# Attention probabilities: six of eight key blocks transposed by DMA, the fp16 cast on ACT, two tiles' PSUM evictions as one

## The reference

```
c_kv = x @ w_dkv; c_q = x @ w_dq
k = concat(rope(x @ w_kr) to all heads, c_kv @ w_uk)      # 16 heads, 64 + 128
q = concat(rope(c_q @ w_qr), c_q @ w_uq)
v = c_kv @ w_uv                                           # 16 heads x 128
attn = softmax(q k^T / sqrt(192)); out = (attn v) @ w_o
x = layernorm(x + out)
w1q, w3q, w2q = ternary(w1), ternary(w3), ternary(w2)     # hidden 682
x = layernorm(x + (silu(x w1q^T) * (x w3q^T)) @ w2q^T)
```

## Time and profile before

| | us |
|---|---|
| median of 3 runs | 1011.03 (1008.86 to 1012.56) |
| the profiled execution | 1020.05 |
| its span in the profile | 1017.9 |
| one pair of heads (300.44 to 343.86) | 43.42 |
| attention, batch 0 and 1 | about 105 to 452 and 584 to 931 |

### The profile page before, as it was taken

The page is one execution under the profiler, slowest core; times in us unless marked ns, Lnnn a source line. Parts: engine busy times, 40 slices in busy tenths (PEclk is TensorE's granted clock), DMA queues, the critical chain, the costliest instruction groups (busy, mean ns, idle before and its releaser), DMA issues.

```text
span 1017.9 us, 18739 instructions
## 1 busy us (share of the span) xinstructions
PE 965.2 (95%) x5622; PEld 696.4 (68%) x5622; DVE 741.0 (73%) x1164; ACT 603.5 (59%) x1036; POOL 605.3 (59%) x643
## 2 busy tenths in 40 slices
PE   7989999999999999998979989999999999997985
PEld 3548766766676766667866866766666676675874
DVE  1756788888888888863456678888888888885455
ACT  2636777777767666751333587766766766764132
POOL 0007777777777777760340787777777777674034
PEclk9799999999999999999989999999999999999998
DMA  9553755545454544566100575655545455457101
GB/s 260 148 217 88 143 103 101 94 95 103 93 96 93 106 94 96 100 140 261 44 23 22 120 129 94 102 100 99 96 89 103 93 97 99 94 103 190 59 1 42
DMA packets 288450, 107.62 MB, mean 106 GB/s; under 512 B 274492, under 2 KB 282512, under 8 KB 287376
## 3 DMA queue, kind: packets, MB, share of 16 engines
q1 hardware_dynamic: 286944, 97.03, 46.1%
q10 hardware_dynamic: 880, 7.86, 2.1%
q0 software_dynamic: 576, 2.10, 0.6%
HBM read 23.85 MB, written 7.60 MB: 31 GB/s over the span
## 4 chain that ended last, share of the span: by engine, by line
PE 73%; issue 10%; DVE 8%; POOL 4%; ACT 2%; DMA 2%; SPq 1%; ACTq 0%; POOLq 0%; DVEq 0%
PE Sa L1045 17%; PE Sb L1045 15%; PE Oa L1072 15%; PE Tb L1054 5%; PE Ta L1054 4%; DVE nmax L753 4%; PE Sb L1096 2%; DVE Q_lo L767 2%; PE Sa L1096 2%; POOL g_lo L415 1%; PE Ob L1082 1%; PE Sb L1172 1%; DMA xr<-in_L_attn_x_dram 1%; POOL P_parts L383 1%; PE Sa L1015 1%
## 5 line engine op out<-in xcount | busy, mean ns | idle before, releaser
L753 DVE TENSOR_REDUCE nmax<-Sa 128x1 f32<-128x1024 f32 x128 | 155.9, 1218 | 78.5 <-PE Sa L1045 77.1
L383 POOL TENSOR_TENSOR P_parts<-probs_a,P_parts 128x512 f16<-128x512 f32 x128 | 169.6, 1325 | 23.5 <-POOL P_parts L380 23.5
L753 DVE TENSOR_REDUCE nmax<-Sb 128x1 f32<-128x1024 f32 x128 | 156.0, 1219 | 20.0 <-PE Sb L1045 20.0
L383 POOL TENSOR_TENSOR P_parts<-probs_b,P_parts 128x512 f16<-128x512 f32 x128 | 149.2, 1166 | 23.9 <-POOL P_parts L380 23.9
L439 ACT ACTIVATE PT_hi<-Ta 128x512 f16<-128x512 f32 x128 | 76.3, 596 | 110.6 <-PE Ta L1054 110.6
L380 POOL TENSOR_SCALAR P_parts<-probs_a 128x512 f16<-128x512 f32 x128 | 80.8, 631 | 75.8 <-ACT probs_a L538 70.4
L380 POOL TENSOR_SCALAR P_parts<-probs_b 128x512 f16<-128x512 f32 x128 | 80.9, 632 | 51.1 <-ACT probs_b L538 48.9
L351 POOL TENSOR_TENSOR turned<-qmul 128x1024 f32<-128x1024 f32 x16 | 38.1, 2404 | 112.2 <-DVE qmul L748 112.2
L1045 PE MATMUL Sb<-K_hi,Q_hi 128*128 128x512 f32 x256 | 91.0, 436 | 7.8 <-ACT probs_b L538 4.0
L1045 PE MATMUL Sa<-K_hi,Q_hi 128*128 128x512 f32 x256 | 93.0, 444 | 0.0
L538 ACT ACTIVATE probs_b<-Sb,nmax 128x1024 f32<-128x1024 f32 x64 | 71.4, 1116 | 33.0 <-DVE nmax L756 33.0
(11 more groups left out here) (298 smaller groups left out, 2118.6 us busy)
## 6 DMA issues: line engine op xcount, KB each, us to landing
QO<-turned SPq DMA_DIRECT2D x64, 128.0 KB, 2.3
TT<-ternary SPq DMA_DIRECT2D x2, 2304.0 KB, 11.5
PT_dma<-P_parts SPq DMA_TRANSPOSE x256, 3.0
ternary<-tern ACTq DMA_DIRECT2D x1, 2304.0 KB, 8.2
wo<-in_L_attn_w_o_dram SPq DMA_DIRECT2D x4, 512.0 KB, 8.1
xq<-in_L_attn_x_dram SPq DMA_DIRECT2D x2, 1024.0 KB, 9.7
wq_high<-Wq_hi ACTq DMA_DIRECT2D x1, 2048.0 KB, 12.7
Wvo_lo<-wvo_low ACTq DMA_DIRECT2D x2, 1024.0 KB, 5.7
```

Of the source, the lines that this page charges most:

```text
L383: nc.gpsimd.tensor_tensor(P_parts[:, n % DEEP, 1, :], src, P_parts[:, n % DEEP, 0, :], ALU.subtract).then_inc(part_lo, 1)
L753: nc.vector.tensor_reduce(nmax[:, n % 4:n % 4 + 1], SS[n % 2][:, :], AX.X, ALU.max, negate=True).then_inc(row_max, 1)
```

## The change

- KP = 2 key blocks stay with TensorE, KD = 6 go by DMA. `transpose_probs` makes two turns a tile instead of four, and two tiles share one PSUM bank (Ta for tiles 0 and 1, Tb for 2 and 3, and so on). ACT evicts and DVE subtracts once for two tiles, after the odd one, 512 columns as before.
- The fp16 cast of the DMA's blocks, now 768 columns, moves from POOL (`split_probs`) to ACT (`part_high`), behind the exponential of the next tile. With it moves the wait for the DMA transpose of four tiles before. POOL keeps the subtraction, of 768 columns (`low_probs`).
- A DMA transpose has 12 blocks instead of 8. TensorE waits for the transposes of a half at key block 2 instead of 4, which is after tile 3 or 11 instead of 5 or 13.
- `P_parts` is larger and reaches into the first four tiles of Wq_lo. These go to HBM in the setup (`wq_low`, 0.5 MB, after waits for `prod_lo` and `qr_lo`) and come back behind Wq_hi after batch 0. Some buffers lie elsewhere.
- The waits that POOL had ahead of the first pair (`q_ps`, `wq_out`) are now waits of ACT at its tile 0 (`wq_out`, `rope_sum`).

```diff
 
 
 DEEP = 4
-KD = KT // 2
+KP = 2
+KD = KT - KP
+SPILL = 4
 EXP0, PT0, PTL0, PV0, OUT0, ROW0, Y0, STORED0, READ0 = 2, DEEP, 2, 2, 1, 1, 2, 1, 1
 
 
...
     ternary = nc.dram_tensor("ternary", [P, W], F, kind="Internal").ap()
 
     wq_high = nc.dram_tensor("wq_high", [P, H * 2 * P], F, kind="Internal").ap()
+    wq_low = nc.dram_tensor("wq_low", [P, SPILL * 2 * P], F, kind="Internal").ap()
     wvo_low = nc.dram_tensor("wvo_low", [P, PAIRS * D], F, kind="Internal").ap()
 
     ctx = ExitStack()
...
                 sp.dma_start(tcos[:, :], cos).then_inc(proj_in, 16)
                 sp.dma_start(tsin[:, :], sin).then_inc(proj_in, 16)
                 if b:
-                    sp.wait_ge(wq_in, 16)
+                    sp.wait_ge(wq_in, 32)
                     sp.sem_inc(wq_ready, 1)
                 for g in range(GROUPS):
                     if g == 3:
...
                 if b + 1 < B:
                     for r in range(DEEP):
                         sp.wait_ge(part_in[r], 16 * TILES * PAIRS // DEEP)
-                    sp.wait_ge(wq_out, 16)
+                    sp.wait_ge(wq_out, 32)
                     sp.dma_start(Wq_hi[:, :, :, :].rearrange("p h c m -> p (h c m)").bitcast(F), wq_high).then_inc(wq_in, 16)
+                    sp.dma_start(Wq_lo[:, 0:SPILL].rearrange("p h c m -> p (h c m)").bitcast(F), wq_low).then_inc(wq_in, 16)
 
 
         @block.gpsimd
...
                     else:
                         nc.gpsimd.tensor_copy(O_parts[:, pair_row, cols], QO[:, pair_row + 1, cols]).then_inc(out_hi, 1)
 
-                def split_probs(tile, n, reused):
-
-                    src = probs[n % DEEP][:, KD * P:S]
-                    hold(pool, exp_done, EXP0 + tile + 1)
-                    if reused is not None:
-                        hold(pool, part_in[n % DEEP], reused)
-                    nc.gpsimd.tensor_scalar(P_parts[:, n % DEEP, 0, :], src, 1.0, 1.0, ALU.mult,
-                                            ALU.mult).then_inc(part_hi, 1)
+                def low_probs(tile, n):
+
                     hold(pool, part_hi, tile + 1)
-                    nc.gpsimd.tensor_tensor(P_parts[:, n % DEEP, 1, :], src, P_parts[:, n % DEEP, 0, :],
-                                            ALU.subtract).then_inc(part_lo, 1)
+                    nc.gpsimd.tensor_tensor(P_parts[:, n % DEEP, 1, :], probs[n % DEEP][:, KP * P:S],
+                                            P_parts[:, n % DEEP, 0, :], ALU.subtract).then_inc(part_lo, 1)
 
                 def pair_pool(p, first, last):
                     pair = b * PAIRS + p
                     for n in range(TILES):
                         h = n // 8
-                        split_probs(pair * TILES + n, n,
-                                    None if first and n < DEEP else 16 * (pair * TILES // DEEP + n // DEEP))
+                        low_probs(pair * TILES + n, n)
                         if n % 8 == 0 and not (first and h == 0):
                             widen(pair * 2 + h - 1, 1 - h)
                         if n % 8 == 1 and not first:
                             high_out(pair * 2 + h - 2, p * 2 - 2, h, False)
 
-                pool.wait_ge(q_ps, b * 4 * GROUPS + 4 * GROUPS)
-                pool.wait_ge(wq_out, 16)
                 pair_pool(0, True, False)
                 with pool.Fori(1, PAIRS) as p:
                     pair_pool(p, False, False)
...
             act_.dma_start(ternary, tern[:, :].bitcast(F)).then_inc(ff_out, 16)
             act_.wait_ge(prod_hi, PAIRS)
             act_.wait_ge(qr_hi, 4)
+            act_.wait_ge(prod_lo, PAIRS)
+            act_.wait_ge(qr_lo, 4)
+            act_.dma_start(wq_low, Wq_lo[:, 0:SPILL].rearrange("p h c m -> p (h c m)").bitcast(F)).then_inc(wq_out, 16)
             act_.dma_start(wq_high, Wq_hi[:, :, :, :].rearrange("p h c m -> p (h c m)").bitcast(F)).then_inc(wq_out, 16)
 
             with act_.Fori(0, B) as b:
...
                             split_high(a, b * PAIRS, a, None)
 
 
+                def part_high(tile, n, reused):
+                    act_.wait_ge(exp_done, EXP0 + tile + 1)
+                    if reused is not None:
+                        act_.wait_ge(part_in[n % DEEP], reused)
+                    copy(P_parts[:, n % DEEP, 0, :], probs[n % DEEP][:, KP * P:S]).then_inc(part_hi, 1)
+
                 def transposed_high(tile, n):
                     act_.wait_ge(pt_ps, PT0 + tile + 1)
-                    dst = PT_hi[:, 1 - n // 8, n // 4 % 2, :, n % 4 * P:n % 4 * P + P]
-                    copy(dst, TS[n % 2][:, :].rearrange("p (k q) -> p k q", k=KD)).then_inc(pt_hi, 1)
+                    dst = PT_hi[:, 1 - n // 8, n // 4 % 2, :, n % 4 // 2 * 2 * P:(n % 4 // 2 + 1) * 2 * P]
+                    copy(dst.rearrange("p k (t q) -> p t k q", t=2),
+                         TS[n // 2 % 2][:, :].rearrange("p (t k q) -> p t k q", t=2, k=KP)).then_inc(pt_hi, 1)
 
                 def row_out(group):
                     act_.wait_ge(row_ps, group + 1)
...
                     pair = b * PAIRS + p
                     t0 = pair * TILES
                     for n in range(TILES):
-                        if first and n == 1:
-                            act_.wait_ge(wq_out, 16)
+                        if first and n == 0:
+                            act_.wait_ge(wq_out, 32)
+                            act_.wait_ge(rope_sum, b * 2 * GROUPS + 2 * GROUPS)
                         if not (last and n == TILES - 1):
                             exponent(t0 + n + 1, n + 1)
                         else:
...
                             act_.wait_ge(lat_out, b * 8 * GROUPS + 8 * GROUPS)
                             for j in range(2):
                                 act_.wait_ge(turned_out[j], b * 64 * GROUPS + 64 * GROUPS)
-                        transposed_high(t0 + n, n)
+                        part_high(t0 + n, n, None if first and n < DEEP else 16 * (t0 // DEEP + n // DEEP))
+                        if n % 2:
+                            transposed_high(t0 + n, n)
                         if n in (3, 11) and not (first and n == 3):
                             row_out(pair * 2 + (n // 8) - 1)
                         if n in (10, 14) and not last:
...
                     pair_act(p, False, False)
                 pair_act(PAIRS - 1, False, True)
                 row_out(b * PAIRS * 2 + 2 * PAIRS - 1)
-
 
                 def x1_high(h):
                     act_.wait_ge(x1T_ps, b * 2 + h + 1)
...
                     nc.vector.tensor_scalar(nmax[:, n % 4:n % 4 + 1], nmax[:, n % 4:n % 4 + 1], PROB_UP_LOG, None,
                                             ALU.add).then_inc(max_ready, 1)
 
-                def transposed_low(tile, n):
-                    dve.wait_ge(pt_hi, tile + 1)
-                    place = (slice(None), 1 - n // 8, n // 4 % 2, slice(None), slice(n % 4 * P, n % 4 * P + P))
-                    nc.vector.tensor_tensor(PT_lo[place], TS[n % 2][:, :].rearrange("p (k q) -> p k q", k=KD),
-                                            PT_hi[place], ALU.subtract).then_inc(pt_lo, 1)
+                def transposed_low(tile2, n):
+                    dve.wait_ge(pt_hi, tile2 + 1)
+                    place = (slice(None), 1 - n // 8, n // 4 % 2, slice(None),
+                             slice(n % 4 // 2 * 2 * P, (n % 4 // 2 + 1) * 2 * P))
+                    nc.vector.tensor_tensor(PT_lo[place].rearrange("p k (t q) -> p t k q", t=2),
+                                            TS[n // 2 % 2][:, :].rearrange("p (t k q) -> p t k q", t=2, k=KP),
+                                            PT_hi[place].rearrange("p k (t q) -> p t k q", t=2),
+                                            ALU.subtract).then_inc(pt_lo, 1)
 
                 def split_low(tile, pair, a):
                     dve.wait_ge(q_split_hi, pair * 2 + a + 1)
...
                                 reciprocal(pair * 2 + h - 1, 1 - h)
                         if not (last and n >= TILES - 2):
                             maximum(t0 + n + 2, n + 2)
-                        transposed_low(t0 + n, n)
+                        if n % 2:
+                            transposed_low(pair * (TILES // 2) + n // 2, n)
                         if n % 8 == 3 and not first:
                             low_out(pair * 2 + h - 2, p * 2 - 2, h)
                         if n in (12, 15) and not last:
...
                                       start=(k == 0), stop=(k == 2))
                     last.then_inc(scores_ready, 1)
 
-                def transpose_probs(tile, n, waited):
+                def transpose_probs(tile, tile2, n, waited):
                     if not waited:
                         pe.wait_ge(exp_done, EXP0 + tile + 1)
-                    pe.wait_ge(pt_lo, tile + 1)
-                    for k in range(KD):
-                        last = nc.tensor.transpose(TS[n % 2][:, k * P:(k + 1) * P],
+                    if n % 2 == 0:
+                        pe.wait_ge(pt_lo, tile2 + 1)
```

(15 more changed lines are left out.)

22 lines of the change are left out of this document (11 added, 11 removed).

## The result

The changed kernel takes 1031.77 us (median of 4 runs, 1030.26 to 1033.79) against 1011.79 for the kernel before on the same chip (4 runs, 1008.86 to 1016.16): a ratio of 1.0195, 95% interval 1.0153 to 1.0237. It is slower, by 20 us. The prediction was 1027.8.

What follows compares the result with a forecast made beforehand. TensorE, busy 95% of the span, was taken as the bound. Stalls of 5.09 us over 39.60 made a pair 44.69, 1.26 more; with edges +16.8 us, so 1027.8, range 1014 to 1038 (8 in 10: 988 to 1038).

Steps and rivals of the forecast that it cites:

- The floor: A steady head pair on TensorE without stalls: eight cycles of 4.84 us and 0.88 for row sums, 39.60 us.
- The lock: SBUF port shared by DVE and POOL: four DVE operations a pair wait for POOL's subtraction, costing 2.64 us.
- The slots: Cycles of two query tiles, each named by its even tile; their stalls in a pair sum to 5.09 us.
- slot 12: Cycle of tiles 12 and 13: row and Q copies on ACT one cycle earlier free bank Sb late, 0.93 us.
- slot 14: Cycle of tiles 14 and 15: line 774 and Q_lo, held by POOL, delay DVE's maximum and bank Sb, 1.49 us.
- slot 0: First cycle of the next pair: late ACT and Q_lo held by POOL delay the maximum and bank Sa, 1.80 us.
- The ACT row: ACT's exponentials, casts and eviction, 4.12 us a cycle: bank Sb is free at 5.02, wanted at 5.06, so just fits.
- First and last tiles: A batch's first eight tiles gain nothing; the first pair's second half gains 1.1 us, the last pair 0.5.
- The end of a batch: Path through last exponential, POOL's subtraction, last transpose and xr load: 2.2 us later, bounds 0.9 and 3.6.
- Transposes: DMA transposes of 12 blocks on SP: issue 1.85 us, landing about 4, hidden; rival that they take over, chance 0.04.
- The total: Whole run: +8.2 us per batch, twice, and 0.5 once, +16.8 us; added to the runs' median, 1027.8.
- half of it: Rival: one Q_lo gets through or DVE's lateness is absorbed; 43.4 us a pair, 1004 to 1016, chance 0.15.

Runs made afterwards that it cites:

- e5d: Changed kernel with DVE's two-input subtractions ahead of the eviction's low part, low output at tiles 3 and 13, Q_lo at 11 and 15: 996.52 us, ratio 0.9841.
- e4: Changed kernel with ACT's copy of the row sums moved from tiles 3 and 11 to 4 and 12: 1020.73 us, ratio 1.0049.
- e10c: Changed kernel with each tile's two turned blocks evicted and subtracted by themselves instead of two tiles as one: 1027.47 us, ratio 1.011.
- e2: Changed kernel with ACT casting only 256 of the 768 columns from a batch's second pair on: 994.49 us, ratio 0.9787.
- e6: Changed kernel with the load of xr issued ahead of the turn of tile 14 in a batch's last pair: 1022.54 us, ratio 1.0075.
- second profile of before: The kernel before, unchanged, run once more for another profile: 1013.74 us, span 1011.5.
- e3: Changed kernel with DVE's two-input subtractions ahead of the low part, low output at tiles 3 and 11, Q_lo at 13 and 15: 1041.32 us, ratio 1.022.
- mended version: Changed kernel with DVE's subtractions reordered, ACT's row copies at tiles 4 and 12, and xr issued earlier: 983.38 us, ratio 0.9685 to the kernel before.

## Why the prediction was right, point by point

- **The floor.** Right: without stalls a pair is 8 x 4.82 + 0.88 = 39.44, predicted 39.60. Turns are 0.22.
- **The cast** took 0.84, predicted 0.82. **POOL's subtraction** took 1.66, not 1.75.
- **The lock.** Right as a mechanism, and in its two numbers: 0.54 after POOL's end for the low output (0.55), 1.00 for what follows Q_lo (1.00). It was to hold four operations a pair; the low output's median is 1.254 and every Q_lo is at 1.784 or more. Its price of 2.64 a pair was probably too high: taking DVE's waits away by order (e5d) gives 2.06, a short POOL 1.54, and neither run removes the lock and nothing else. By the rule of the Trainium skill ("SBUF — State Buffer", section "SBUF: two separate sides") the one that starts second waits for the whole of the other's instruction, and the runs agree on both sides: DVE's Q_lo 2.60 behind POOL, POOL's subtraction 2.47 behind DVE.
- **The slots.** Predicted and measured stall: slot 4 0.39, 0.16; slot 6 0.48, 0.38; slot 12 0.93, 1.14; slot 14 1.49, 0.88; slot 0 1.80, 1.67; slot 2 0, 0.28; slots 8 and 10 nothing in both. In all 5.09 and 4.51. The rise per pair was +0.54, predicted +1.26: the sign held with little to spare. The term that was off most is slot 14, 1.49 against 0.88. Slot 12 is near its number for another reason than the one given: Sb's scores wait there only 0.34 (at 315.69) of the 0.66 put down for the copies on ACT, and the next pair's first scores, which end the slot, wait 0.42 for Q_lo (at 319.41), a wait that the sum did not have. With TensorE that much later and POOL 0.09 shorter, Sb's scores in slot 14 (at 321.89) wait 0.62 and not 1.22. e4, without the row copy, has 0.62 left in slot 12, 0.44 of it for Q_lo. Slot 2's 0.28 was put at nothing; with the shorter evictions of e10c it is 0.06.
- **The ACT row**, with Sb's exponential fitting by 0.04: right as a warning. e2 shows that a shorter cast alone removes 2.74, more than the lock's share. The prediction put 3.29 of 5.09 on the slots of Q_lo; it didn't see that slot 0's share halves when the cast is shorter.
- **First and last tiles.** The first eight tiles went at 4.40 a cycle for bank Sb, as predicted, and at 4.50 for Sa, 0.2 us more in all. The first pair's second half was to gain 1.1; from the first maximum to the scores of slot 0 it gained 0.1. The step put a stall of 0.93 in all there, none of it in slot 14, since no low output stands ahead of it. Slot 14 had 0.89 all the same: Q_lo at tile 12 ran into a POOL subtraction that had begun 0.27 before it and took 2.46. With the normalisation behind the second Q_lo, the first pair loses 1.6 by normalisations, and the last one gains 0.8: together +0.8 a batch in place of -1.6.
- **The end of a batch.** Predicted +2.2 each, bounds 0.9 and 3.6. Measured +3.8 from the last exponential to xr's issue, against the first profile of before, and +3.6 against the mean of the four ends: at its upper bound or 0.2 beyond. The path through ACT and POOL came about as worked out: POOL ended 5.37 after that exponential's start and not 3.48, 1.9 later where 2.2 was predicted. The issue of a turn behind a load was left at its old length, and it is the term that grew, by the other 1.9: 4.88 and 1.44 for the last two turns, where the last took 3.03 before. e6 shows it: xr ahead of them gives 6.5 us a batch back.
- **Transposes.** Their issue took 1.43, not the 1.85 by proportion, and landed in 3.7, not 4. TensorE waited for one of them 0.2 us in the whole run. Hidden, as predicted.
- **The total.** +16.8 was predicted between spans. Between the after and the second profile of before it is +17.1, but of other terms: the pairs +6.5 where +15.1 was predicted, the rest +10.6 where +1.7 was. In the runs' medians it is +20.0, and against the first profile of before, to whose span the 16.8 were added, +10.7. So the time is right to 0.4% by luck in good part: the pairs' rise was forecast at more than twice its size, and edges put too small made up for it. What the runs bear out is the direction and the mechanism, a stall behind the port and a full ACT, whose rise of 4.2 a pair is larger than the turns' 3.7.

Of the rivals, "half of it" (43.4 a pair) lay nearer in the pair than the forecast did, 0.56 against 0.73 away.

## What to carry to other kernels

When work leaves the busiest engine and its helpers are within a few hundredths of its cycle, the gain goes to whichever shared thing two helpers meet at; write down who arrives first there, because whoever comes second waits for the other's whole instruction. Here only the order of DVE's instructions decided between 1.0195 and 0.9841, and putting an operation ahead pays only if its input and its reader's deadline both allow it (e3 against e5d). Try the reordering on the old kernel as well: most of the gain of the mended version was there without the change, and two thirds of what could be placed there came from issuing one load earlier.
